# Second sample's first layer norm split over ScalarE, GpSimd and VectorE in an adapter + mixture-of-experts kernel

## What is computed

```python
# stage 0: domain adapter
hidden = gelu(einsum('bsd,ad->bsa', x, down_W) + down_b)            # A = 32
hidden = einsum('bsa,boa->bso', hidden, expert_W[dom]) + expert_b[dom] + domain_emb[dom]
x0     = einsum('bsa,da->bsd', hidden, up_W) + up_b + x
mu, var = mean(x0, -1), mean((x0 - mu) ** 2, -1)
x1     = (x0 - mu) * rsqrt(var + 1e-5) * ln_gamma + ln_beta         # the "first layer norm"
# stage 1: mixture of experts with a style-conditioned norm
h      = layer_norm(x1) * ln_g + ln_b                               # over the features
h      = (h - mean(h, tokens)) * rsqrt(var(h, tokens) + 1e-8)       # over the 256 tokens
h      = h * softplus(gamma[subject]) + beta[subject]
gates  = top-2 of softmax(h @ router_w), scaled to sum 1            # E = 8 experts
y      = sum_e gates[e] * (relu(h @ w1[e] + b1[e]) @ w2[e] + b2[e]) # FF = 512
return x1 + y
```

## Time and profile before

| | |
|---|---|
| time, median of 3 runs | 125.7 us (121.97, 125.70, 128.08) |
| profiled execution | 121.37 us, of which 119.6 us are the span from its first to its last instruction |
| busy in the span | PE 112.3 us (94%), DVE 91.9 us (77%), ACT 84.6 us (71%), POOL 54.2 us (45%) |
| first expert matmul (L588) starts at | 19.38 us |

### The profile page before, as it was taken

One profiled execution on the slowest core, in us unless ns is written; L12 is line 12 of the kernel. 1 busy time (PEld: TensorE's weight loads), 2 busy tenths in 40 slices (PEclk: granted clock), 3 DMA queues, 4 the chain that ended last, 5 costly groups with the idle time before them and its releaser, 6 DMA issues.

```text
span 119.6 us, 1660 instructions
## 1 busy us (share of the span) xinstructions
PE 112.3 (94%) x518; PEld 84.9 (71%) x518; DVE 91.9 (77%) x229; ACT 84.6 (71%) x153; POOL 54.2 (45%) x75
## 2 busy tenths in 40 slices
PE   6989978899997999999999999999999999999990
PEld 2457535556884888788888888888888888888780
DVE  4856989998599969987777759595958677776871
ACT  2157753898899797786878787878787787878300
POOL 5200999045117000101049999997668941321300
PEclk9999999999999999999999999999999999999999
DMA  2998299991000000144999600000000000000006
GB/s 79 374 215 334 56 455 431 375 414 41 0 0 3 0 5 0 21 163 138 356 407 419 266 0 5 0 0 0 0 0 0 0 0 0 5 0 0 0 0 175
DMA packets 4472, 14.17 MB, mean 118 GB/s; under 512 B 560, under 2 KB 1904, under 8 KB 4208
## 3 DMA queue, kind: packets, MB, share of 16 engines
q1 hardware_dynamic: 3024, 9.67, 22.5%
q0 software_dynamic: 1008, 3.67, 8.7%
q10 hardware_dynamic: 432, 0.73, 1.8%
HBM read 13.52 MB, written 0.56 MB: 118 GB/s over the span
## 4 chain that ended last, share of the span: by engine, by line
PE 70%; DVE 18%; ACT 4%; issue 3%; DMA 2%; POOL 1%; DVEq 0%; ACTq 0%; POOLq 0%
PE bank L588 21%; PE bank L589 21%; PE bank L627 11%; PE bank L607 10%; DVE hid_low L995 3%; DMA ids_i<-ids_dram 2%; DVE x L897 2%; ACT hid_high L502 2%; DVE stats L904 1%; ACT bank L505 1%; PE bank L582 1%; PE bank L567 1%; DVE bank L889 1%; POOL z L365 1%; PE bank L577 1%
## 5 line engine op out<-in xcount | busy, mean ns | idle before, releaser
L502 ACT ACTIVATE hid_high<-bank,early_sb 128x512 fp32r<-128x512 f32 x64 | 44.2, 691 | 16.6 <-PE bank L607 16.5
L995 DVE TENSOR_TENSOR hid_low<-bank,hid_high 128x512 fp32r<-128x512 f32 x51 | 34.8, 688 | 17.3 <-ACT bank L505 16.5
L505 ACT ACTIVATE bank<-bank,early_sb 128x512 f32<-128x512 f32 x51 | 33.5, 658 | 0.0
L303 POOL TENSOR_TENSOR w_low<-w_raw,w_high 128x256 fp32r<-128x256 f32 x32 | 22.8, 737 | 15.5 <-ACT w_high L490 6.1
L588 PE MATMUL bank<-hid_high,w_low 128*128 128x512 f32 x64 | 25.7, 402 | 0.8 <-DVE y_raw L1005 0.8
L627 PE MATMUL bank<-hid_low,w_high 128*128 128x512 f32 x64 | 25.8, 403 | 0.8 <-DVE hid_low L995 0.4
L588 PE MATMUL bank<-h_high,w_low 128*128 128x512 f32 x64 | 25.6, 399 | 0.3 <-ACT h_high L480 0.3
L589 PE MATMUL bank<-h_high,w_high 128*128 128x512 f32 x64 | 25.4, 396 | 0.0
L607 PE MATMUL bank<-h_low,w_high 128*128 128x512 f32 x64 | 25.0, 396 | 0.0
L589 PE MATMUL bank<-hid_high,w_high 128*128 128x512 f32 x64 | 25.0, 391 | 0.0
L313 POOL TENSOR_TENSOR y_sum<-y_sum,y_part 128x512 f32<-128x512 f32 x9 | 11.6, 1294 | 16.7 <-DVE y_part L1015 14.7
(11 more groups left out here) (136 smaller groups left out, 104.4 us busy)
## 6 DMA issues: line engine op xcount, KB each, us to landing
w_high<-w_all_dram POOLq DMA_DIRECT2D x7, 512.0 KB, 7.8
w_raw<-w_all_dram SPq DMA_DIRECT2D x1, 2560.0 KB, 10.7
gate_all<-gate_scratch SPq DMA_DIRECT2D x4, 512.0 KB, 6.2
gate_all<-gate_scratch SPq DMA_DIRECT2D x1, 2048.0 KB, 13.2
w_raw<-w_all_dram SPq DMA_DIRECT2D x3, 512.0 KB, 7.8
style_sb<-style_dram SPq DMA_DIRECT2D x1, 324.0 KB, 4.6
tables_sb<-tables_dram ACTq DMA_DIRECT2D x1, 272.0 KB, 3.0
xT_sb<-xT_dram SPq DMA_DIRECT2D x1, 256.0 KB, 3.6
```

Source lines behind the costliest of these rows:

```text
L303: nc.gpsimd.tensor_tensor(w_low[:, e % W_RING, quarter(q)], w_raw[:, e, quarter(q)], w_high[:, e % W_RING, quarter(q)].bitcast(F32), ALU.s ...
L502: ac(hid_high[:, slot, :], hid_ps[slot][:, :], ACT.Relu, bias=bias).then_inc(relu_steps, 1)
L505: ac(hid_ps[slot][:, :], hid_ps[slot][:, :], ACT.Relu, bias=bias).then_inc(relu_steps, 1)
L995: v.tensor_tensor(low, ps, high.bitcast(F32), ALU.subtract).then_inc(low_vector, 1)
```

## The change

All of it lies in the front part, for sample 1 (tiles 2 and 3). `centre(1)` and `adapter_out(1)`, four DVE instructions, go. In their place: DVE makes the shift -mean * rstd of both tiles in one small instruction (`shift_sum`); ACT makes (sum - mean) * rstd of each tile from PSUM into `x_norm` with scale and bias by partition; POOL multiplies by gamma into `x_gain`; DVE adds beta into `x1` (`add_bias`).

The lists are put in another order around it. On DVE `x1_shift(0)` now stands ahead of `x1_stats(1)`, and `minus_abs` behind `token_mv(1, 1)`. On ACT the two `x_norm` stand ahead of the rounding of expert 0's weights; the root of sample 0 moves ahead of `gamma_raw` and `beta_T`; the root of sample 1 moves ahead of the softplus's exponential. On POOL the two products stand ahead of everything, and the four subtractions for expert 0 move from ahead of `normalise(0, T)` to behind it.

```diff
--- before.py
+++ after.py
@@ -141,6 +141,9 @@
         gamma_g = sb("gamma_g", [P, B])
         g2 = sb("g2", [P, 1])
         x1 = sb("x1", [P, J, D])
+        sum_shift = sb("sum_shift", [P, T])
+        x_norm = sb("x_norm", [P, T, D])
+        x_gain = sb("x_gain", [P, T, D])
         stats = sb("stats", [P, 2, J, 6])
         mv = sb("mv", [P, 2, J, 2])
         log_var = sb("log_var", [P, 2, J])
@@ -213,6 +216,7 @@
         gamma_beta_ready = sem("gamma_beta_ready")
         soft_in, soft_exp, soft_ln = sem("soft_in"), sem("soft_exp"), sem("soft_ln")
         centred, sum_taken = sem("centred"), sem("sum_taken")
+        sum_shifted, sum_normed, sum_gained = sem("sum_shifted"), sem("sum_normed"), sem("sum_gained")
         var_ready, log_ready, rstd_ready = sem("var_ready"), sem("log_ready"), sem("rstd_ready")
         z_affine, z_ready, zT_in_psum = sem("z_affine"), sem("z_ready"), sem("zT_in_psum")
         z_vector, z_scalar = sem("z_vector"), sem("z_scalar")
@@ -377,8 +381,12 @@
 
             pool.wait_ge(early_loaded, 16)
             load_high(1)
+            pool.wait_ge(ln0_loaded, 16)
+            for t in range(T):
+                pool.wait_ge(sum_normed, t + 1)
+                nc.gpsimd.tensor_tensor(x_gain[:, t, :], x_norm[:, t, :], ln0_sb[:, 0, :], ALU.mult).then_inc(sum_gained, 1)
+            normalise(0, T)
             split_lows(0)
-            normalise(0, T)
             split_lows(1, (0, 1))
             load_high(2)
             load_high(3)
@@ -506,16 +514,20 @@
 
             act.wait_ge(eps_ready, 1)
             token_root(0, tiles(0, 2))
+            act.wait_ge(sum_shifted, 1)
+            for t in range(T):
+                ac(x_norm[:, t, :], sum_ps[1][:, t, :], ACT.Identity, bias=sum_shift[:, t:t + 1],
+                   scale=rstd[:, 0, T + t:T + t + 1]).then_inc(sum_normed, 1)
             round_first_weights((0, 1, 2))
             act.wait_ge(style_in_psum, 4)
             ac(sty1_T[:, :], sty1_ps, ACT.Relu, bias=col(C_SB1, SC)).then_inc(style_ready, 1)
+            token_root(1, tiles(0))
             round_first_weights((3,))
             act.wait_ge(style_in_psum, 6)
             ac(gamma_raw[:, :], gam_ps, ACT.Identity, bias=col(C_SBG)).then_inc(gamma_beta_ready, 1)
             ac(beta_T[:, :], bet_ps, ACT.Identity, bias=col(C_SBB)).then_inc(gamma_beta_ready, 1)
-            token_root(1, tiles(0))
+            token_root(1, tiles(1))
             soft_exponential()
-            token_root(1, tiles(1))
             soft_logarithm()
             normalise(T + 1)
             feature_root(0)
@@ -893,9 +905,20 @@
 
                 ve.wait_ge(rstd_ready, root_of["token", 0, b // HB * HB])
                 for j in tiles(b):
-                    ve.wait_ge(centred, j + 1)
+                    ve.wait_ge(centred, j + 1 - (T if b >= HB else 0))
                     v.scalar_tensor_tensor(x1[:, j, :], sum_ps[b][:, j % T, :], rstd[:, 0, j:j + 1], ln0_sb[:, 1, :],
                                            ALU.mult, ALU.add).then_inc(sum_taken, 1)
+
+            def shift_sum():
+
+                ve.wait_ge(rstd_ready, root_of["token", 0, 0])
+                v.scalar_tensor_tensor(sum_shift[:, :], mv[:, 0, T:2 * T, 0], -1.0, rstd[:, 0, T:2 * T], ALU.mult, ALU.mult
+                                       ).then_inc(sum_shifted, 1)
+
+            def add_bias():
+                for t in range(T):
+                    ve.wait_ge(sum_gained, t + 1)
+                    v.tensor_tensor(x1[:, T + t, :], x_gain[:, t, :], ln0_sb[:, 1, :], ALU.add).then_inc(sum_taken, 1)
 
             def x1_stats(b, between=None):
 
@@ -1023,14 +1046,15 @@
             style_step(2)
             ve.wait_ge(ln0_loaded, 16)
             centre(0)
+            shift_sum()
             adapter_out(0)
-            centre(1)
             x1_stats(0)
-            adapter_out(1)
             token_mv(1, 0)
-            x1_stats(1, between=minus_abs)
+            add_bias()
+            x1_shift(0)
+            x1_stats(1)
             token_mv(1, 1)
-            x1_shift(0)
+            minus_abs()
             normalise(1)
             x1_shift(1)
             softplus(0)
```

## The result

The change is slower: the ratio of its time to that of the kernel before is **1.020**, 95% interval 1.0145 to 1.0263 (medians 126.09 us of 4 runs against 123.91 us of 4). The same kernel timed again gave 1.0203 (1.0157 to 1.0249). That is 2.5 us, where the forecast had 0.9, and it lies on the 2% line itself. Every kernel here also has runs several us longer, at a granted clock of 0.93 to 0.96 of full speed; the ratios and their intervals use only the other runs, of which the change has three (124.36, 124.37, 124.87 us).

The account below looks back on a forecast made before the run. PE, busy 94% of the span, was taken as the bound, with any shift of the first expert matmul reaching the end; 0.55 + 0.1 + 0.25 = +0.9 us gave 126.6 us on the median, range 122.2 to 129.0 us.

Parts of the forecast that it names:

- That it gets slower, and not faster: Whole kernel: +0.9 us forecast, against a rival that VectorE's relief wins, 0.45 us less, chance 0.17.
- What DVE won on sample 0: Front part, first sample: `mv` would end at about 13.30 instead of 14.03, 0.73 us won on DVE.
- DVE and ACT lists, +0.55: Front part: DVE waits for sample 0's root, late in ACT's list, so the second `z_shift` comes 0.55 us later.
- Softplus, +0.1: Front part: DVE's step L831 waits for ACT's second softplus step; 0 to +0.3 us, taken as +0.1.
- POOL's two-input partners, +0.25 out of 0 to 2.1: DVE's small steps `t_gain`, `scale_T`, two `shift_T` may wait out POOL's subtractions; 0 to 2.1 us, taken as +0.25.
- The sign of being wrong: One of three signs set: DVE's steps between 18 and 19.5 us stretch by more than a microsecond.
- Weights late: POOL's `w_low` hidden, nothing counted; as a rival, expert 2's transfer delays sample 2's z tiles, +1.9 us, chance 0.12.
- PE's clock: Start of the expert part: PE, quiet from about 13.1 to 14.75 us, might drop its clock; +3 us, chance 0.06.
- Rival 4: PE's clock falls to 1.2 GHz at the expert part's start, matmuls take twice as long; +3 us, chance 0.06.
- Rival 2: The lock bites: three small DVE steps wait out a subtraction each, 2.1 us, softplus 0.3; +2.95 in all, chance 0.13.

Follow-up runs that it names:

- r4_stats_first: The change with `x1_shift(0)` put behind `token_mv(1, 1)` on DVE, so DVE no longer waits for the first root; ratio 1.0222 to the kernel before.
- r3_before_pool_late: The kernel before with only POOL's order edited: z tiles of samples 0 and 1 ahead of expert 0's four subtractions, no norm split; ratio 1.0208.
- r6_change_clear: The change with one expert 0 subtraction ahead of the z tiles, one behind, then four transfers, a wait for `h_ready` and six subtractions; ratio 1.0048 to the kernel before.
- r1_after_again: The change itself, unaltered, timed and profiled again; ratio 1.0203 to the kernel before, profiled at 124.39 us.

## Why the prediction was right or wrong

The time (126.09 us) lies in the range and near the 126.6 that was forecast, but that nearness is the scatter's; measured as a ratio the loss is 2.5 us and not 0.9. The mechanism of the larger part was named and mis-sized.

- *That it gets slower, and not faster.* Right. What DVE won on sample 0 (`mv` at 13.43 instead of 14.03) was lost in ACT's list, as worked out.
- *DVE and ACT lists, +0.55.* Right in size at its place: 0.50. Whether it reaches the end is not shown. With the wait taken away (1.0222) and with no split at all (1.0208) the ratio is that of the change, and with POOL cleared 0.0048 are left, whose interval holds both nothing and the whole term. The few runs at nearly full clock, 123.78 and 123.88 us with POOL's order alone against 124.19 and 124.36 for the change, rather speak for it.
- *Softplus, +0.1.* `gamma_g` was held 0.66 us instead of 0.24; with full clock it moved the feature statistics by most of 0.37.
- *POOL's two-input partners, +0.25 out of 0 to 2.1.* This is the step that failed. It was 1.46, nearly six times the term. Of that, in `r4_stats_first`, `t_gain` and `scale_T` lost 0.97, and the two `t_off`, which have one input and which I had not counted, 0.50; the two `shift_T` had POOL's block behind them and lost nothing. The sign of being wrong that I had set, more than a microsecond of stretch in these steps, came. I took the low end because L913 and L831 had taken 0.16 us beside POOL's z tile. That row did not bear it: the first of them started at 15.38 and ended at 15.54, 0.01 us behind the z tile's end at 15.53, so there was hardly anything left to wait for. The one row that showed a collision at length (0.65 against 0.41 us) should have set the value.
- *`h_low`.* Not in the sum, though it was the very row that showed the lock. It cost 0.61, and PE waited for it.
- *Weights late.* Right to count nothing: PE waited for no `w_low` in the front part.
- *PE's clock.* It fell in both profiles of the change, in the second behind the stretch in which PE waits for the style column. But `r4_stats_first` has that wait too, kept the full clock and lost the same 2.5 us, so the clock is not the cause. The change's own runs say the same: 124.19 and 124.36 us at 0.999 and more, 124.37 to 124.87 at 0.972 to 0.986. A small fall does go with POOL's block behind the z tiles: ten of the fifteen runs behind the four ratios of the change (timed twice), of `r3_before_pool_late` and of `r4_stats_first` had 0.972 to 0.986, and none of 24 such runs of the kernel before was under 0.996. What it costs was isolated by no experiment (0.2 us apart in the change, 0.8 in `r3_before_pool_late`). Rival 4's half speed at the start of the expert part was seen only in the profiles of the two runs with added POOL work, where PE had waited over 3 us (3.10 and 3.15).
- *Rival 2* was what happened, with 1.46 + 0.37 + 0.61 in place of my 2.1 + 0.3. I gave it 0.13.

The Trainium skill, "SBUF — State Buffer", section "Who interferes with whom", has the rule as the runs show it: a VectorE instruction with two SBUF inputs collides with a GpSimd instruction that reads SBUF and not with one that only writes, and a `tensor_scalar` in a 2-port mode collides with either. The runs agree on the first: 0.16 us beside memsets, 0.66 beside subtractions. `gamma_g`, a `tensor_scalar`, was held by both (4.17 and 0.66); that it was in such a mode no trace shows. Another `tensor_scalar` of four columns with input and output in SBUF was not held: in the kernel before it began and ended within POOL's second z tile (15.64 to 16.10).

```profile
15.67 0.17 DVE L835 TENSOR_SCALAR gamma_T<-gamma_T 128x4 f32<-128x4 f32 x1
```

Why it got by stays open.

## What to carry to other kernels

When a change moves work on POOL, ask which small DVE steps on the critical chain will then run beside it: each one that reads two SBUF tiles while POOL reads SBUF can last until POOL's instruction is over, and so can a step that scales a tile in SBUF (`gamma_g` and `t_off` did, L835 did not). Long POOL work belongs where DVE reads PSUM (the statistics `t_stats` took 0.43 us beside POOL's subtractions before, `h_full` 0.54 in `r4_stats_first` partly beside them and 0.54 in `r6_change_clear` without them), or behind a wait for the end of the chain; a block of it must not begin when the chain is about to enter its two-column steps. And an operator split over three engines is worth only what its last tile comes earlier, which here was nothing (2.87 us before, 2.86 in the change).

## What the runs showed of the hardware that I had not expected

- A `tensor_scalar` of 128x4 that met six back-to-back memsets on POOL waited for all of them, 4.17 us, while against back-to-back subtractions DVE's steps were let in after one or two (0.64 to 0.82 us). It was one run; why the two differ stays open.
- A wait of this kind is quantised. The step ends some 0.02 us behind POOL's instruction (`scale_T` 21.20, POOL's block 21.18), so a chain of such steps moves at POOL's pace. A step that starts just before the end of a subtraction waits for the next one too: `t_off` in `r1_after_again` started at 19.33, 0.10 us before a subtraction ended, and ended at 20.15, behind the next one, which ran from 19.39 to 20.11.
- POOL is held as well: with DVE's two `h_low` beside them, two subtractions took 1.64 us in `r4_stats_first` (from 22.27) where they took 1.42 before.
